# Routing four groups at a time, scaling x on ScalarE and VectorE, and copying x during the first stage

## The chip, the cores and the metric

One core of one Trainium2 chip runs the whole kernel. The metric is the device time of one execution in microseconds (us): the median of three runs. An engine's name is followed once by its short name in the profile: TensorE (PE; PEld is its weight load), VectorE (DVE), ScalarE (ACT), GpSimd (POOL), SyncE (SP, which here only issues DMAs).

## The reference

```python
# x [128, 64, 256], cond [128, 256], w [256, 256]; then T = 8192 tokens of D = 256, E = 8 experts, F = 1024
ys = y * (1 / sqrt(256))
d = rsqrt(einsum('bi,io->bo', ys * ys, w * w) + EPS)
hidden = einsum('bsi,io->bso', x * ys[:, None, :], w) * d[:, None, :]
logits = hidden @ wr.T                       # [T, 8]
vals, idx = top_k(logits, 2)                 # gating = softmax over the two
mask = (idx[:, :, None] == arange(E)).any(axis=1)
pos = cumsum(mask, axis=0) - 1               # place of a token in its expert's list
keep = mask & (pos < cap)                    # cap = 2560
dispatch[e, slot] = token                    # the list of each expert
h = gelu(xg @ w1[e] + b1[e]);  y = h @ w2[e] + b2[e]
out = x + segment_sum(y * g, dispatch)       # back to the tokens
```

Everything is float32. The order of the tokens matters: the cumulative count runs over all 8192 of them.

## The kernel before

There are two stages. The first makes `hidden` and the routing, for 16 groups of 512 tokens (`GROUPS`, four tiles of 128 each). The second runs the experts, in 46 blocks of 384 slots, each of 8 chunks of the inner dimension.

In the first stage each group passes through these steps.

- SP loads a group of x, transposed, into one of four buffers (`load_x`), and loads the next one into a buffer when `modulate` has read it.
- POOL multiplies it by `ys` in place, in two instructions (`scale_x`, L336), two groups ahead.
- PE multiplies by `w` (`modulate`, L464) into three banks.
- ACT scales the lower half by `d` (`scale_hidden`, L672, eight small instructions), DVE the upper half (L810).
- PE turns the group back to token rows and computes the logits at once (`turn_back`, L477 and L479); ACT copies the four tiles into `rows` (`copy_back`, L657).

The routing works on a set of two groups (`PAIR = 2`, so 8 tiles and 8 sets). DVE takes the two largest logits and their experts (`choose`, L820 to L834, a chain of small instructions, each of which waits for the one before). The difference goes to ACT for an exponential (`odds`, L662), and DVE makes the two gates (`set_gates`, L839 to L845) right behind `choose`. POOL writes the gates into `rows` (`weigh_gates`, L344 to L349), and SP stores the set to `hidden` in DRAM (`store_rows`). PE counts positions (`positions`, L489 to L500), DVE turns them into slot numbers (`find_slots`, L852 to L869), and for each group writes one-hot tiles (`list_group`, L876 and L890) that PE multiplies into the lists (`list_slots`, L511). VectorE's program is a loop over groups g: `scale_hidden(g)`; at even g `list_group(g-3)`, `choose` and `set_gates` of the set that ends with g-1; at odd g `find_slots` and `list_group(g-3)`; and for g from 3 to 10 one piece of the first expert's weights is split (`split_piece`, L779 on DVE, L648 on ACT). PE's is `modulate(g)`, at odd g `positions`, `turn_back(g-1)`, `list_slots(g-4)`.

At the end POOL works out what is added to the lists (`base_ids`, L371 to L380), DVE adds it (`ids`, shown as L790, a helper's line) and POOL gathers the rows of block 0 (`gather`, L391). SP loads the weights of expert 1 when the first expert's are split, and when all groups are listed it loads `b2` and issues 16 copies of x into the output (`copy_x`, L280), to which the second stage adds. PE transposes a gathered block (`transpose_block`, L537) and starts the products (L547 to L561). ACT applies gelu (L701), and in the first two blocks of an expert it also splits the next expert's weights, waiting for them before the first piece.

Of the kernel before, what the change touches and what calls it, by code (L numbers as in the profile page):

```python
# [30 lines left out]
PAIR = 2  # L31
SETS = GROUPS // PAIR
TS = PAIR * TILES
X_RING = 4
ROW_RING = 4
# [34 lines left out]
def build(nc, x, x_t, cond_t, w, wr_t, w1, b1_t, w2, b2, ident, tri, expert_low, slot_base, middle_ids, lanes,  # L70
# [9 lines left out]
    with ExitStack() as ctx:  # L80
# [36 lines left out]
        base_ids = sb("base_ids", [P, E, TILES_E])  # L117
# [15 lines left out]
        first = [sb(f"first{u}", RE) for u in range(2)]  # L133
        second = [sb(f"second{u}", RE) for u in range(2)]
# [9 lines left out]
        gate = [sb(f"gate{u}", [P, 2, TS]) for u in range(2)]  # L144
        picked = sb("picked", [P, 2, TS, E])
        weighed = sb("weighed", [P, 2, TS, E])
# [40 lines left out]
        set_act = sem("set_act")  # L187
        w_loaded = sem("w_loaded")

        x_loaded = [sem(f"x_loaded{i}") for i in range(X_RING)]  # L190
        xs_ready = sem("xs_ready")
# [11 lines left out]
        gates_ready = sem("gates_ready")  # L203
        gates_weighed = sem("gates_weighed")
# [3 lines left out]
        halves_known = sem("halves_known")  # L208
        half_saved = sem("half_saved")
        base_step = sem("base_step")  # L210
        base_ready = sem("base_ready")
# [63 lines left out]
        def _(sp):  # L275
# [14 lines left out]
            for g in range(1, X_RING):  # L290
                load_x(g)
            sp.wait_ge(set_dve, 1)
# [11 lines left out]
            for g in range(X_RING, GROUPS):  # L304
# [25 lines left out]
        def _(pool):  # L330
            def scale_x(g):

                pool.wait_ge(x_loaded[g % X_RING], 16 * (g // X_RING + 1))
                for k in range(KC):
                    cols = x_in[g % X_RING][:, k, :].rearrange("p (b s) -> p b s", s=S)
                    pool.tensor_tensor(cols, cols, ys_t[:, k, g * GB:(g + 1) * GB].unsqueeze(2).to_broadcast([P, GB, S]),  # L336
                                       ALU.mult).then_inc(xs_ready, 1)

            def weigh_gates(s):

                pool.wait_ge(gates_ready, s + 1)
                if s > 0:
                    pool.wait_ge(rows_ready, s)
# [11 lines left out]
            for g in range(GROUPS):  # L355
                if g + 2 < GROUPS:
                    scale_x(g + 2)
# [90 lines left out]
        def _(pe):  # L448
# [70 lines left out]
            for g in range(1, GROUPS):  # L519
# [6 lines left out]
                if g >= 4:  # L526
                    list_slots(g - 4)
# [539 lines left out]
```

## Time and profile before

| what | us |
|---|---|
| median of 3 runs | 1011.01 (1010.73 to 1012.35) |
| profiled execution, whole | 1011.03 |
| its span, first to last instruction | 1008.8 |
| PE busy | 935.2 (93%) |
| ACT busy | 511.7 (51%) |
| DVE busy | 489.3 (49%) |
| POOL busy | 439.5 (44%) |

The profile shows one execution. Times are from the span's start. The chain of work that ended last is followed back from the last instruction; 84% of it is PE. Busy time of PE says less than it seems, since matmuls are pipelined and their ends are modelled; the start of one to the start of the next is the measure that counts. The same holds for DVE and ACT: an instruction's duration includes a part that overlaps with the next.

### The profile page before, as it was taken

To read this page: it belongs to the slowest core of one execution; us is meant where nothing else is said; L and a number is where in the kernel's file an instruction comes from. 1 tells how busy PE (TensorE), PEld (TensorE's weight loads), DVE (VectorE), ACT (ScalarE), POOL (GpSimd) and SP (SyncE) were. 2 spreads that over 40 slices of the span, in tenths; PEclk is the share of its full clock that TensorE was granted. 3 is DMA by queue.
4 is the path that set the end of the run, shared out by engine and by line. 5 is a ranking of instruction groups with operands and counts; after the bars stand their busy time and mean duration, and the time that the engine had idled before them with its cause. 6 is when DMAs were issued, how large, how long until landed. Compare 5 with 4: busy or idle time off the path is not lost.

```text
span 1008.8 us, 19314 instructions
## 1 busy us (share of the span) xinstructions
PE 935.2 (93%) x6398; PEld 889.5 (88%) x6399; DVE 489.3 (49%) x1152; ACT 511.7 (51%) x1106; POOL 439.5 (44%) x480
## 2 busy tenths in 40 slices
PE   6887861999999999999999999999999999999994
PEld 3454540999999999999999999999999999999994
DVE  3678683453554346443544455345444544344441
ACT  3543330565565556555655556556455655545551
POOL 4142213253544545454454535445453544545433
PEclk9999985899999999999999999999999999999997
DMA  8434229552244323523252325323432232322322
GB/s 271 113 106 146 66 93 354 182 131 37 51 76 101 47 38 52 122 49 47 48 130 37 50 39 131 47 48 46 120 50 41 48 47 44 48 37 52 42 33 32
DMA packets 53466, 82.04 MB, mean 81 GB/s; under 512 B 6656, under 2 KB 42496, under 8 KB 53056
## 3 DMA queue, kind: packets, MB, share of 16 engines
q0 software_dynamic: 26496, 36.76, 23.3%
q1 hardware_dynamic: 25392, 44.42, 13.5%
q10 hardware_dynamic: 1552, 0.53, 0.2%
q8 instruction: 13, 0.21, 0.1%
q14 instruction: 13, 0.11, 0.0%
HBM read 54.16 MB, written 35.93 MB: 89 GB/s over the span
## 4 chain that ended last, share of the span: by engine, by line
PE 84%; DVE 9%; DMA 3%; issue 2%; POOL 1%; ACT 1%; SPq 0%; POOLq 0%; DVEq 0%
PE bank L559 13%; PE bank L560 13%; PE bank L561 13%; PE bank L548 13%; PE bank L547 13%; PE bank L549 13%; PE bank L537 3%; DMA sb_xg<-hidden,sb_gather_ids 2%; PE bank L464 1%; PE bank L477 1%; PE bank L479 1%; DVE sb_h_raw L890 1%; DVE sb_h_raw L876 1%; DVE sb_hid_t L810 1%; DVE sb_picked L860 1%
## 5 line engine op out<-in xcount | busy, mean ns | idle before, releaser
L969 DVE TENSOR_TENSOR sb_h_lo<-sb_h_raw,sb_h_hi 128x384 fp32r<-128x384 f32 x368 | 205.2, 558 | 321.5 <-ACT sb_h_hi L701 321.5
L701 ACT ACTIVATE sb_h_raw<-bank,sb_b_now 128x384 f32<-128x384 f32 x368 | 214.8, 584 | 282.2 <-PE bank L549 282.0
L559 PE MATMUL bank<-sb_w_hi,sb_h_hi 128*128 128x256 f32 x1104 | 315.1, 285 | 0.0
L560 PE MATMUL bank<-sb_w_lo,sb_h_hi 128*128 128x256 f32 x1104 | 311.6, 282 | 0.0
L561 PE MATMUL bank<-sb_w_hi,sb_h_lo 128*128 128x256 f32 x1104 | 310.1, 281 | 0.0
L404 POOL DMA_INDIRECT out_rows<-sb_y,sb_add_ids x138 | 222.8, 1614 | 67.8 <-POOL sb_add_ids L401 38.0
L547 PE MATMUL bank<-sb_xt_hi,sb_w_hi 128*128 128x384 f32 x736 | 250.0, 340 | 1.7 <-issue 1.7
L548 PE MATMUL bank<-sb_xt_lo,sb_w_hi 128*128 128x384 f32 x736 | 249.9, 340 | 0.0
L549 PE MATMUL bank<-sb_xt_hi,sb_w_lo 128*128 128x384 f32 x736 | 249.6, 339 | 0.0
L701 ACT ACTIVATE sb_h_hi<-bank,sb_b_now 128x384 fp32r<-128x384 f32 x368 | 212.3, 577 | 0.0
L561 PEld LDWEIGHTS bank<-sb_w_hi,sb_h_lo 128*128 128x128 f32 x1104 | 208.4, 189 | 0.0
L559 PEld LDWEIGHTS bank<-sb_w_hi,sb_h_hi 128*128 128x128 f32 x1104 | 208.0, 188 | 0.0
L560 PEld LDWEIGHTS bank<-sb_w_lo,sb_h_hi 128*128 128x128 f32 x1104 | 207.6, 188 | 0.0
L391 POOL DMA_INDIRECT sb_xg<-hidden,sb_gather_ids x138 | 136.8, 992 | 67.4 <-POOL sb_ids_ring L387 39.1
L547 PEld LDWEIGHTS bank<-sb_xt_hi,sb_w_hi 128*128 128x128 f32 x736 | 138.8, 189 | 2.1 <-issue 2.1
L548 PEld LDWEIGHTS bank<-sb_xt_lo,sb_w_hi 128*128 128x128 f32 x736 | 138.9, 189 | 0.0
L549 PEld LDWEIGHTS bank<-sb_xt_hi,sb_w_lo 128*128 128x128 f32 x736 | 138.9, 189 | 0.0
L386 POOL COPY sb_gather_ids<-sb_ids 128x3 int32 (+1 forms) x46 | 11.3, 247 | 265.6 <-DVE sb_gates L937 263.1
L690 ACT CAST sb_xt_hi<-bank 128x384 fp32r<-128x384 f32 x92 | 39.6, 483 | 111.3 <-PE bank L549 81.6
L928 DVE TENSOR_TENSOR sb_xt_lo<-bank,sb_xt_hi 128x384 fp32r<-128x384 f32 x92 | 47.1, 553 | 95.1 <-ACT sb_xt_hi L690 95.1
L994 DVE TENSOR_TENSOR sb_y<-bank,sb_b 128x256 f32<-128x256 f32 x138 | 50.1, 419 | 43.4 <-PE bank L561 43.4
L464 PE MATMUL bank<-sb_x,sb_w 128*128 128x512 f32 x128 | 63.8, 646 | 1.4 <-ACT sb_hid_t L672 1.4
(113 smaller groups left out, 622.0 us busy)
## 6 DMA issues: line engine op xcount, KB each, us to landing
sb_w_raw<-in_w SPq DMA_DIRECT2D x16, 1024.0 KB, 8.3
hidden<-sb_rows SPq DMA_DIRECT2D x8, 1056.0 KB, 6.3
sb_x<-in_x_t SPq DMA_DIRECT2D x16, 512.0 KB, 4.2
out_rows<-in_x SPq DMA_DIRECT2D x16, 512.0 KB, 14.1
sb_xg<-hidden,sb_gather_ids POOLq DMA_INDIRECT x138, 2.8
out_rows<-sb_y,sb_add_ids POOLq DMA_INDIRECT x138, 3.8
sb_b<-in_b SPq DMA_DIRECT2D x1, 1024.0 KB, 5.7
hidden<-sb_empty SPq DMA_DIRECT2D x3, 132.0 KB, 8.2
```

Of the source, the lines that this page charges most:

```text
L391: pool.indirect_dma_start(xg[:, s, :], None, hidden, bass.IndirectOffsetOnAxis(gather_ids[:, s:s + 1], axis=0),).then_inc(gathered, 16)
L404: pool.indirect_dma_start(out, bass.IndirectOffsetOnAxis(add_ids[:, s:s + 1], axis=0), y[s][:, :], None, compute_op=ALU.add,).then_inc(add ...
L464: mm = pe.matmul(m_bank[c % M_RING][:, :], w_sb[:, k, o * P:(o + 1) * P], x_in[g % X_RING][:, k, :], start=(k == 0), stop=(k == KC - 1))
L547: pe.matmul(h, w_hi[u][:, cols], xt_hi[:, rows], start=(k == 0), stop=False)
L548: pe.matmul(h, w_hi[u][:, cols], xt_lo[:, rows], start=False, stop=False)
L549: mm = pe.matmul(h, w_lo[u][:, cols], xt_hi[:, rows], start=False, stop=(k == KC - 1))
L559: pe.matmul(y, hi, w_hi[u][:, cols], start=(f == 0), stop=False)
L560: pe.matmul(y, hi, w_lo[u][:, cols], start=False, stop=False)
L561: mm = pe.matmul(y, lo, w_hi[u][:, cols], start=False, stop=(f == FC - 1))
L701: ins = act.activation(h, h_bank[f % H_BANKS][:, 0:SLOTS], ACT.Gelu_apprx_tanh, bias=b1_now[u][:, f:f + 1])
L969: dve.tensor_tensor(h_lo[f % RING][:, :], h_raw[f % RING], h_hi[f % RING][:, :].bitcast(F32), ALU.subtract).then_inc(h_ready, 1)
L994: dve.tensor_tensor(y[s][:, :], y_bank[s][:, 0:D], b2_sb[:, bass.ds(e * D, D)], ALU.add).then_inc(y_read, 1)
```

## The change

`JOINED = 4` takes the place of `PAIR = 2`: four groups, 16 tiles, are one set, and there are four sets. The instructions of `choose`, `set_gates`, `find_slots` and `positions` are issued half as often on twice the width; `rows` has two buffers of twice the size. `set_gates` stands a group after `choose`, behind `find_slots`, and DVE also writes the gates to `rows`. The scaling of x leaves POOL: ACT does the lower half in eight small instructions, DVE the upper half in one. DVE also does POOL's work on the list base, after its last group, and `b2` is waited for later. SP issues one copy of x behind each load of x; the load of `b2` and of expert 1's weights now stands behind the first transposes of the second stage (`t_done`). The table of the square root is loaded ahead of its use.

```diff
-PAIR = 2
-SETS = GROUPS // PAIR
+JOINED = 4
+SETS = GROUPS // JOINED
-ROW_RING = 4
+ROW_RING = 2
@@ sync
+            sp.wait_ge(zeros, 1)
...
-                if g % 2 == 0 and g >= 8:
-                    store_rows((g - 8) // 2)
-            for s in range(GROUPS // 2 - 4, SETS):
-                store_rows(s)
+                copy_x(g - X_RING)
+                if g % JOINED == 2 and g >= 2 * JOINED:
+                    store_rows(g // JOINED - 2)
+            store_rows(SETS - 2)
+            for g in range(GROUPS - X_RING, GROUPS):
+                copy_x(g)
+            store_rows(SETS - 1)
+            sp.wait_ge(t_done, 1)
+            sp.dma_start(b2_sb[:, :], b2.rearrange("e d -> (e d)").partition_broadcast(P)).then_inc(b2_in, 16)
             sp.wait_ge(w_lo_done, PIECES)
             load_weights(1)
-            sp.wait_ge(listed, GROUPS)
-            sp.dma_start(b2_sb[:, :], b2.rearrange("e d -> (e d)").partition_broadcast(P)).then_inc(b2_in, 16)
-            for g in range(GROUPS):
-                copy_x(g)
@@ gpsimd: scale_x, weigh_gates and the work on base_ids go
@@ tensor
-                pe.wait_ge(xs_ready, KC * (g + 1))
+                pe.wait_ge(xs_lower, g + 1)
+                pe.wait_ge(xs_upper, g + 1)
...
-                if g >= 3 and g % 2 == 1:
-                    positions((g - 3) // 2)
+                if g % JOINED == 1 and g > JOINED:
+                    positions(g // JOINED - 1)
                 turn_back(g - 1)
-                if g >= 4:
-                    list_slots(g - 4)
+                if g % JOINED == 3 and g > JOINED:
+                    list_slots(g - 7)
+                    list_slots(g - 6)
+                if g % JOINED == 0 and g > JOINED:
+                    list_slots(g - 6)
+                    list_slots(g - 5)
             turn_back(GROUPS - 1)
-            list_slots(GROUPS - 4)
+            list_slots(GROUPS - 6)
+            list_slots(GROUPS - 5)
             positions(SETS - 1)
-            for g in range(GROUPS - 3, GROUPS):
+            for g in range(GROUPS - JOINED, GROUPS):
                 list_slots(g)
@@ scalar
+            def scale_x(g):
+
+                act.wait_ge(x_loaded[g % X_RING], 16 * (g // X_RING + 1))
+                for i in range(GB):
+                    cols = x_in[g % X_RING][:, 0, i * S:(i + 1) * S]
+                    b = g * GB + i
+                    ins = act.mul(cols, cols, ys_t[:, 0, b:b + 1])
+                ins.then_inc(xs_lower, 1)
...
             for g in range(GROUPS):
+                if g + 2 < GROUPS:
+                    scale_x(g + 2)
                 if g + 1 < GROUPS:
                     scale_hidden(g + 1)
+                if g % JOINED == 0 and g > 0:
+                    odds(g // JOINED - 1)
                 copy_back(g)
-                if g % 2 == 0 and g >= 2:
-                    odds(g // 2 - 1)
@@ vector
+            def scale_x(g):
+
+                dve.wait_ge(x_loaded[g % X_RING], 16 * (g // X_RING + 1))
+                cols = x_in[g % X_RING][:, 1, :].rearrange("p (b s) -> p b s", s=S)
+                dve.tensor_tensor(cols, cols, by_batch(ys_t, 1, g), ALU.mult).then_inc(xs_upper, 1)
...
             for g in range(GROUPS):
                 scale_hidden(g)
-                if g == GROUPS // 2 + 4:
-                    dve.wait_ge(listed, GROUPS // 2)
-                    dve.tensor_copy(lower_list[:, :], list_half[0]).then_inc(half_saved, 1)
-                if g % 2 == 0:
-                    if g >= 4:
-                        list_group(g - 3)
-                    if g >= 2:
-                        choose(g // 2 - 1)
-                        counts = set_gates(g // 2 - 1)
-                elif g >= 3:
-                    find_slots((g - 3) // 2, counts)
-                    list_group(g - 3)
+                if g + 2 < GROUPS:
+                    scale_x(g + 2)
                 if 3 <= g < 3 + PIECES:
                     split_piece(0, g - 3, g - 2)
+                if g == GROUPS // 2 + 5:
+                    save_half()
+                if g % JOINED == 0 and g > 0:
+                    choose(g // JOINED - 1)
+                if g % JOINED == 1 and g > JOINED:
+                    find_slots(g // JOINED - 1)
+                    set_gates(g // JOINED - 1)
+                if g % JOINED == 2 and g > JOINED:
+                    list_group(g - 6)
+                    list_group(g - 5)
+                if g % JOINED == 3 and g > JOINED:
+                    list_group(g - 5)
+                    list_group(g - 4)
             choose(SETS - 1)
             set_gates(SETS - 1)
-            list_group(GROUPS - 3)
-            find_slots(SETS - 1, None)
+            find_slots(SETS - 1)
+            for g in range(GROUPS - JOINED, GROUPS):
+                list_group(g)
```

## Rows read from the trace of the kernel before

**Rows 1.** Busy time by stretch: each engine's us (instructions), granted clock, DMA share, GB/s.

```profile
60.39:78.13 17.74, 14.51 (x73) 9.22 (x73) 14.20 (x38) 7.65 (x27) 5.29 (x7) 0.92 0.40 119
...
160.00:190.00 30.00, 12.32 (x66) 11.95 (x67) 6.74 (x17) 8.04 (x17) 6.32 (x8) 0.62 1.00 342
```

**Rows 2.** Timeline of DVE over one set: start, duration, instruction [idle before].

```profile
61.59 0.68 DVE L876 TENSOR_TENSOR sb_h_raw<-sb_lanes,sb_lane_of 128x1024 f16<-128x1024 f16 x1
...
63.56 0.22 DVE L820 TENSOR_REDUCE sb_top<-sb_rows 128x8 f32<-128x64 f32 x1
...
66.38 0.22 DVE L834 TENSOR_TENSOR sb_mask<-sb_first,sb_second 128x64 bf16<-128x64 f32 x1
69.57 0.17 DVE L839 TENSOR_SCALAR sb_gate<-sb_ratio 128x8 f32<-128x8 f32 x1 [2.96 <-ACT sb_ratio L662]
...
70.74 0.68 DVE L810 TENSOR_TENSOR sb_hid_t<-bank,sb_d_t 128x512 f32<-128x512 f32 x1
71.34 0.22 DVE L852 TENSOR_SCALAR sb_over<-bank 128x64 f32<-128x64 f32 x1
...
76.15 0.69 DVE L876 TENSOR_TENSOR sb_h_raw<-sb_lanes,sb_lane_of 128x1024 f16<-128x1024 f16 x1
```

**Rows 3.** Timeline of POOL over the same set.

```profile
71.58 4.08 POOL L336 TENSOR_TENSOR sb_x<-sb_x,sb_ys_t 128x512 f32<-128x512 f32 x4
```

**Rows 4.** Timeline of DVE where POOL no longer scales x.

```profile
139.88 0.21 DVE L852 TENSOR_SCALAR sb_over<-bank 128x64 f32<-128x64 f32 x1
...
141.92 0.69 DVE L876 TENSOR_TENSOR sb_h_raw<-sb_lanes,sb_lane_of 128x1024 f16<-128x1024 f16 x1
```

**Rows 5.** Timeline of PE in the same set as Rows 2.

```profile
66.66 0.20 PE L495 MATMUL bank<-sb_mask,sb_tri 128*128 128x64 bf16 x1 [0.48 <-DVE sb_mask L834]
...
66.91 0.47 PE L477 MATMUL bank<-sb_back,sb_hid_t 128*128 128x136 f32 x2
...
68.85 1.38 PE L511 MATMUL bank<-sb_b,sb_h_raw 128*128 128x168 f16 x8
70.05 3.61 PE L464 MATMUL bank<-sb_x,sb_w 128*128 128x512 f32 x8
73.50 0.40 PE L477 MATMUL bank<-sb_back,sb_hid_t 128*128 128x136 f32 x2
```

**Rows 6.** Timeline of ACT in the same set.

```profile
72.04 1.75 ACT L672 ACTIVATE sb_hid_t<-bank,sb_d_t 128x64 f32<-128x64 f32 x8 [2.00 <-PE bank L464]
74.16 1.77 ACT L657 COPY sb_rows<-bank 128x264 f32<-128x264 f32 x4 [0.37 <-PE bank L479]
```

**Rows 7.** Timeline of DVE at the start.

```profile
6.33 1.34 DVE L759 TENSOR_TENSOR sb_wsq<-sb_w 128x512 f32<-128x512 f32 x1
...
15.39 0.42 DVE L771 TENSOR_TENSOR sb_d_t<-sb_tmp_t,sb_root_t 128x256 f32<-128x256 f32 x1
```

**Rows 8.** Timeline of PE: the last matmuls of the last `turn_back`.

```profile
141.76 0.40 PE L479 MATMUL bank<-sb_back,sb_hid_t 128*128 128x136 f32 x2
```

**Rows 9.** Timeline of DVE: the list is complete.

```profile
158.96 0.33 DVE L790 TENSOR_TENSOR sb_ids<-bank,sb_base_ids 128x168 int32<-128x168 f32 x1 [1.58 <-PE bank L511]
```

**Rows 10.** Timeline of SP's queue: the issue of the 16 copies of x.

```profile
159.24 10.59 SPq L280 DMA_DIRECT2D out_rows<-in_x x16
```

**Rows 11.** The chain that ended last: block 0's gather from its last issue, and its transposes.

```profile
163.38 12.52 DMA sb_xg<-hidden,sb_gather_ids
175.94 1.55 PE bank L537 x6
```

**Rows 12.** The page's DMA issues: count, KB each, median us from issue to landing.

```profile
hidden<-sb_rows SPq DMA_DIRECT2D x8, 1056.0 KB, 6.3
...
sb_xg<-hidden,sb_gather_ids POOLq DMA_INDIRECT x138, 2.8
```

**Rows 13.** Timeline of ACT in block 0: its first piece of expert 1's weights.

```profile
185.24 0.62 ACT L648 CAST sb_w_hi<-sb_w_raw 128x512 fp32r<-128x512 f32 x1
```

**Rows 14.** Timeline of PE in block 0: the product of chunk 6 starts.

```profile
190.47 0.34 PE L547 MATMUL bank<-sb_xt_hi,sb_w_hi 128*128 128x384 f32 x1
```

More of the change, by code:

```diff
@@ L132, in build @@
         hit = sb("hit", RE)
-        first = [sb(f"first{u}", RE) for u in range(2)]
-        second = [sb(f"second{u}", RE) for u in range(2)]
+        chosen = sb("chosen", [P, 2, TS, E])
+        first, second = chosen[:, 0, :, :], chosen[:, 1, :, :]
         mask = sb("mask", RE, BF16)
@@ L143, in build @@
         ratio = sb("ratio", [P, TS])
-        gate = [sb(f"gate{u}", [P, 2, TS]) for u in range(2)]
+        gate = sb("gate", [P, 2, TS])
         picked = sb("picked", [P, 2, TS, E])
-        weighed = sb("weighed", [P, 2, TS, E])
         slot_of = sb("slot_of", [P, 2, TS])
@@ L330, in _ @@
         def _(pool):
[L331 to L343, printed above, removed]
-                pool.tensor_tensor(weighed[:, 0, :, :], first[s % 2][:, :, :],
-                                   gate[s % 2][:, 0, :].unsqueeze(2).to_broadcast(RE), ALU.mult)
-                pool.tensor_tensor(weighed[:, 1, :, :], second[s % 2][:, :, :],
-                                   gate[s % 2][:, 1, :].unsqueeze(2).to_broadcast(RE), ALU.mult).then_inc(gates_weighed, 1)
-                pool.wait_ge(gates_weighed, s + 1)
-                pool.tensor_tensor(rows[s % ROW_RING][:, :, GATE_AT:GATE_AT + E], weighed[:, 0, :, :],
-                                   weighed[:, 1, :, :], ALU.add).then_inc(rows_ready, 1)
@@ L640, in _ @@
             act.dma_start(lane_sb[:, :, :], lanes.rearrange("p (n j) -> p n j", j=TILES)).then_inc(const_in, 16)
+            act.wait_ge(zeros, 1)
+            act.activation(warm_sb[:, :], empty_sb[:, 0:1], ACT.Sqrt)
+            def scale_x(g):
[5 more added lines that the diff above has]
+                ins.then_inc(xs_lower, 1)
+            act.wait_ge(set_dve, 2)
+            scale_x(0)
+            scale_x(1)
             act.wait_ge(set_dve, 5)
@@ L823, in choose @@
                 after(mark(dve.tensor_reduce(low[:, 0, :], hit[:, :, :], AX_X, ALU.min)))
-                after(mark(dve.tensor_tensor(first[s % 2][:, :, :], low3, over_e(low[:, 0, :]), ALU.is_equal)))
-                after(mark(dve.scalar_tensor_tensor(rest[:, :, :], first[s % 2][:, :, :], -BIG, logits,
+                after(mark(dve.tensor_tensor(first, low3, over_e(low[:, 0, :]), ALU.is_equal)))
+                after(mark(dve.scalar_tensor_tensor(rest[:, :, :], first, -BIG, logits,
                                                     ALU.mult, ALU.add)))
@@ L990, in one_block @@
                     split_chunk(b + 1, 0)
+                if isinstance(b, int) and b == 0:
+                    dve.wait_ge(b2_in, 16)
                 for s in range(SUBS):
```

114 lines of the change are left out of this document (50 added, 64 removed).

## The prediction

> **What bounds the kernel now.** I read the busy time by stretch first. From 200 us on PE never idles and the change touches nothing there, so the question is how early the second stage starts. In the first stage [rows 1], over one set of two groups (17.74 us), DVE is busy 14.20, PE's records 14.51 at a granted clock of 0.92, ACT 7.65. That settles nothing, so I followed DVE's timeline through the set [rows 2], from start to start: `list_group` 1.97 (61.59 to 63.56), `choose` 3.04 (63.56 to 66.60), idle 2.96 for ACT's exponential, `find_slots` 4.81 (71.34 to 76.15), `scale_hidden` 0.60. With the second list, the second hidden, two weight pieces (0.60 each) and gates (0.57) that is 17.7: DVE's own order fills the period, 8.87 us a group. Two parts are not work. The 2.96 us is a wait: ACT's exponential stands behind `copy_back`, that behind PE's `turn_back`, that behind `positions`, which waits for the mask (0.48) [rows 5]. And `find_slots` takes 4.81 beside POOL's four scalings of x [rows 3], but 2.04 where POOL has none [rows 4]: 2.77 us.
>
> PE's own work [rows 5]: `modulate` 3.45 (70.05 to 73.50), `turn_back` 1.94 at most (66.91 to 68.85; 1.85 by its steps of 0.23), `list_slots` 1.20 (68.85 to 70.05), `positions` 0.25 a set of two. So 6.6 us a group: DVE costs 2.2 us a group over PE.
>
> The end of the stage: the last `turn_back` ends at 142.0 [rows 8] (141.76 plus its second half), the list is complete at 159.3 [rows 9], and then block 0's gather takes 12.52 us from its last issue [rows 11], while all 16 copies of x go out from 159.24 [rows 10] and the DMA engines are full, 342 GB/s [rows 1]. The same gather lands in 2.8 us as a rule [rows 12]. PE stands still for all of it.
>
> **DVE after the change.** A small instruction of `choose` steps by 0.25 us; 64 more elements at DVE's pace, read off the 0.60 us step of a 512-element one and the 0.25 step of a 64-element one (448 elements, 0.35 to 0.45 us), are 0.06. Per set of four groups: `choose` 3.04 + 12 x 0.06 = 3.8; `find_slots` 2.04 + about 0.8 = 2.8 (two 64-wide products become one of 256); gates with the two instructions that were POOL's 1.45; four lists 7.9; four `scale_hidden` 2.4; four halves of `scale_x` at the same width 2.4; weight pieces 2.4. Sum 23.2, and 20.8 once the pieces are done: 5.8 and 5.2 us a group. The exponential has a whole group of time, so the 2.96 goes; POOL is silent, so the 2.77 goes.
>
> **PE sets the pace then.** Per four groups: 4 x (3.45 + 1.85 + 1.20) = 26.0, and `positions` for 16 tiles. That is 1216 columns in place of 352 (sum of its matmul widths) against 0.25 us: 0.6 to 0.9, I take 0.6. So 26.6 us per set of four, 6.65 a group, uneven: 5.3, 5.9, 7.7, 7.7, since lists come at g mod 4 = 3 and 0. Does anything miss its turn? The mask of a set: its last rows are copied 5.9 us into iteration 4k, `choose` ends at 9.8, and `positions` is asked at 7.7 + 3.45 = 11.1: 1.3 us spare, but for the first set, with no lists yet, 1.0 late. Lists are made by 23.3 and asked at 24.2.
>
> **ACT.** Hidden 8 x 0.20 = 1.62 (the 1.75 of [rows 6] less the tail), `copy_back` 1.66, and the new `scale_x`. No row shows a 64-wide scaling out of SBUF. Bounds: as out of PSUM, 1.62, or without any overlap at 0.33 each, 2.66. I take 1.62, the same form on the same engine. Then 4.9 a group, 5.4 with a weight piece: under 6.65, but even with PE's 5.3 in groups that have no lists.
>
> **The start.** `wsq` takes 1.34 beside POOL [rows 7], and 0.68 is what a product of that width takes alone [rows 2]; two of the 256-wide steps on the way to `d` are slowed likewise. Against that ACT must scale groups 0 to 2 itself before hidden. I take `d` 2.4 us earlier than 15.8, and after ACT's added 1.7 us `modulate(2)` at 19.5 instead of 21.3.
>
> **The first stage summed.** `modulate(2)` at 19.5. Groups 2 to 6 at 5.4 to 5.6 (ACT and PE even), with the first `positions` 0.6 and its late mask 1.0: `modulate(7)` at 48.3. Then 7.7, 7.7, 5.9, 5.4, 7.7, 7.7, 5.9, 5.4: `modulate(15)` at 101.7, its iteration's end 109.4, last `turn_back` 111.3. Before, 142.0. Saved 30.7.
>
> **The tail** grows. From the end of that `turn_back`: copy 0.7, `choose` 3.8, gates 1.5, `find_slots` 3.0 with its wait for `positions`, four lists 7.9 where two stood, PE's last list 1.4, the `ids` 0.5: 18.8. DVE's five steps for the base fit beside the last list. Before it was 159.3 - 142.0 = 17.3. Net 29.2: the list is complete at 130.1.
>
> **The gather.** The rows of the last set must be stored first. That store is 2.1 MB, issued at about 117.3; the 1056 KB one lands in 6.3 [rows 12], and another 1.1 MB at 342 GB/s or at half of that adds 3.2 to 6.3, so it lands between 126.8 and 130. The first gather is issued at 131.4: hidden by 1.4 to 4.6 us. With the copies gone, the gather lands in 2.8 instead of 12.5: 9.7 saved. Landing of block 0's rows: 175.9 - 29.2 - 9.7 = 137.0.
>
> The Trainium skill, "DMA: Bandwidth & Descriptors", § Queues, rings and completion order, says that a DMA's semaphore increment lands only after every earlier write of that DMA engine, across its queues. By it the 12.5 us is the wait behind copies that were issued before the gather, and [rows 10, 11] fit; it would also put the gather behind the store of the last set, should that be late.
>
> **A new wait in block 0.** SP now issues `b2` (1 MB) and expert 1's weights (2 MB) behind the first transposes, which end 1.6 us after the landing [rows 11]. With block 1's rows 3.55 MB go out; at 342 GB/s 10.4 us, and up to 2.8 more for completion: they are there 12.5 to 15.3 us after the landing. ACT wants them 9.3 after it (185.24) [rows 13], so it stalls 3 to 6 us. PE wants the gelu behind that piece at 14.6 (190.47) [rows 14], and ACT needs 0.5 + 1.1 us from the weights to it: late by 0 to 2.3. I take 1.4; later pieces are not late. The `b2` wait of DVE is later still and costs nothing.
>
> **Sum.** 1008.8 - 29.2 - 9.7 + 1.4 = 971.3 of span. Around the span the profiled execution has 2.2 us (1011.03), and it stands at the median (1011.01): 973.5, I say 974.
>
> **Rivals.**
> 1. *ScalarE becomes the bound.* For it: only 0.1 to 0.5 us spare in groups without lists. If a scaling out of SBUF costs up to 0.33 us, ACT takes 6.4 with a weight piece and 5.9 without. Groups 2 to 6 then cost 4 to 5 us more, and each later short pair 0.5 to 1 us: 6 in all, 980; the full bound gives 984. Against: ACT has 1 to 2 us spare in each pair of 7.7.
>    The Trainium skill, "VectorE: DVE Perf Modes", § The TRN2 errata, gives ScalarE 224 fixed cycles from SBUF and 172 from PSUM; as an estimate from that page, 43 ns on each of 128 instructions, 5.5 us of ACT, would by this rival's reckoning make it some 976 to 977. No row here can show it.
> 2. *The gather was not held by the copies* but by its own first use or by the last store, which is now twice as large: the 9.7 us stays. 974 + 9.7 = 984. The change would not do that half of what it says. Against: [rows 1, 10].
> 3. *Transfers bound the first stage.* One queue now carries load, copy and store: 0.52 + 0.52 + 0.54 MB = 1.6 MB a group. At 342 GB/s that is 4.7 us, under 6.65. But a store of 1056 KB in 6.3 us is no more than 170 GB/s, completion included [rows 12]. Stores alone at that rate and the rest at 342 make 6.3 us: still under. Should it be at 220 GB/s throughout, 7.3 us a group: 8 us more, 982 to 990.
> 4. *Slower than before.* The same mechanism further on: every x load stands behind a copy and a store, and all traffic runs at the store's 170 GB/s. From 1.6 MB / 9.3 us, that is under 172 GB/s, the first stage eats the whole 37 us; at 160 GB/s it is 10 us a group, 1021. Against: 342 GB/s with 16 copies in flight [rows 1].
> 5. *Better than I count:* DVE and ACT start earlier and no weights stall: 963 to 968.
>
> **How the numbers follow.** Forecast (966 to 979) 0.60; ScalarE bound (979 to 984) 0.14; gather unchanged (984) 0.07; transfers (982 to 990, a tail above) 0.10; slower 0.02; better 0.07. A measurement of this kernel tells about 0.2% (2 us) from no change. The range 966 to 986 leaves out the better case, the slower one and most of the tail, 0.15 or so. Faster 0.97, same 0.01, slower 0.02.
>
> **What would show it.** PE's waits in the first stage all but gone, clock near 1.00, `modulate` to `modulate` at 5.3, 5.9, 7.7, 7.7; `modulate(15)` near 102; DVE waiting for PE; the list complete near 130; the gather landing in about 3 us; ACT waiting 3 to 6 us for weights in block 0. Wrong if: ACT has no idle time in groups 2 to 8 (rival 1); DVE or ACT waits for loads of x (3, 4); the last issue of the first gather to its landing stays near 12 (2); or the set's mask, not PE, releases `positions` in each set.

## The result, and the profile after

The changed kernel takes 976.02 us, the median of four executions (974.30 to 976.37), against 1011.27 for the kernel before on the same chip. The ratio is 0.9647, with a 95% interval of 0.9630 to 0.9663: 35 us faster. The profiled execution took 976.05, its span is 974.2 (before: 1008.8). The forecast of 974 was 2 us low, and the range held the result.

Where the 34.6 us of span come from: the list is complete at 134.7 instead of 159.3 (24.6 us), and block 0's rows land 6.8 us after that, where they took 16.6 before (9.8). From the landing to the end both kernels take the same, 832.7 and 832.9.

First the view by stretch of the kernel after, which answers [rows 1]. Its columns: stretch, length, then busy us (instructions) of PE, PEld, DVE, ACT and POOL, granted clock of TensorE as a share of 2.4 GHz, DMA share, GB/s.

```profile
42.70:47.09 4.39, 4.19 (x33) 4.19 (x34) 1.34 (x3) 1.84 (x5) 0.00 (x0) 0.61 0.55 212
47.09:114.50 67.41, 67.41 (x358) 44.74 (x357) 56.07 (x131) 51.73 (x201) 0.00 (x0) 1.00 0.61 206
```

From 47.09 to 114.50, ten iterations, PE is never idle and its clock is granted in full: 6.74 us a group, where it was 8.87. DVE is busy 83% and ACT 77% of it, so both still have room. The first row is the one stretch in the middle of the stage where this fails; it comes back below.

The timeline of PE of the kernel after, one set of four groups, `modulate` (L411) from start to start, and the set's first count of positions (L442), which answer [rows 5]. Columns: start, duration, instruction, tiles, [idle before].

```profile
60.56 3.61 PE L411 MATMUL bank<-sb_x,sb_w 128*128 128x512 f32 x8
...
68.30 3.62 PE L411 MATMUL bank<-sb_x,sb_w 128*128 128x512 f32 x8
...
71.75 0.22 PE L442 MATMUL bank<-sb_mask,sb_tri 128*128 128x128 bf16 x1
...
74.27 3.17 PE L411 MATMUL bank<-sb_x,sb_w 128*128 128x512 f32 x7
```

The steps are 7.74 and 5.97 (the last line is short because its view ends there), and `positions` waits for nothing, since DVE has written the mask 0.3 us before it is asked (71.17 and 0.29 long, next fence). The timeline of DVE of the kernel after over `choose` of the same set, against [rows 2]:

```profile
67.61 0.28 DVE L797 TENSOR_REDUCE sb_top<-sb_rows 128x16 f32<-128x128 f32 x1
...
71.17 0.29 DVE L811 TENSOR_TENSOR sb_mask<-sb_chosen 128x128 bf16<-128x128 f32 x1
72.02 0.69 DVE L789 TENSOR_TENSOR sb_hid_t<-bank,sb_d_t 128x512 f32<-128x512 f32 x1 [0.56 <-PE bank L411]
```

`choose` for 16 tiles takes 3.8 us (67.61 to 71.38), as forecast, and behind it DVE waits for PE: the roles have changed. No wait for the exponential is left.

The chain that ended last of the kernel after, in order of time, from the first gather to the first transposes, against [rows 11]:

```profile
136.02 1.17 POOL sb_xg L337
...
138.77 2.72 DMA sb_xg<-hidden,sb_gather_ids
141.50 0.04 issue
141.54 1.54 PE bank L489 x6
```

The gather lands 2.72 us after its last issue, where it took 12.52.

### The profile page after: what moved, and what is told of

It is laid out like the page before. It is cut to its first block, busy times and chain, and to the rows that moved or that the text cites. A ratio compares the mean times of both kernels' runs of the same rounds, so it can differ in the third digit from the quotient of the medians.

```text
span 974.2 us, 19276 instructions
## 1 busy us (share of the span) xinstructions
PE 932.7 (96%) x6402; PEld 891.0 (91%) x6403; DVE 470.1 (48%) x1068; ACT 539.6 (55%) x1231; POOL 390.7 (40%) x419
## 4 chain that ended last, share of the span: by engine, by line
PE 84%; issue 14%; POOL 1%; DMA 0%; DVE 0%; POOLq 0%; DVEq 0%
PE bank L511 14%; PE bank L512 14%; PE bank L513 13%; PE bank L499 13%; PE bank L500 13%; PE bank L501 13%; PE bank L489 3%; POOL out_rows L350 0%; DMA sb_xg<-hidden,sb_gather_ids 0%; POOL sb_xg L337 0%; DVE sb_y L997 0%; DVE sb_y L1003 0%; POOL sb_add_ids L347 0%; POOL sb_gather_ids L332 0%; POOL sb_ids_ring L333 0%
## 5 line engine op out<-in xcount | busy, mean ns | idle before, releaser
L511 PE MATMUL bank<-sb_w_hi,sb_h_hi 128*128 128x256 f32 x1104 | 314.8, 285 | 0.0
L511 PEld LDWEIGHTS bank<-sb_w_hi,sb_h_hi 128*128 128x128 f32 x1104 | 207.8, 188 | 0.0
L411 PE MATMUL bank<-sb_x,sb_w 128*128 128x512 f32 x128 | 59.5, 608 | 0.5 <-ACT sb_hid_t L639 0.4
```

The source lines that it names most:

```text
L411: mm = pe.matmul(m_bank[c % M_RING][:, :], w_sb[:, k, o * P:(o + 1) * P], x_in[g % X_RING][:, k, :], start=(k == 0), stop=(k == KC - 1))
L511: pe.matmul(y, hi, w_hi[u][:, cols], start=(f == 0), stop=False)
```

## The experiments

Each time below is a median with the range of its runs, beside the kernel before on the same chip (1011.8 to 1012.4 in the four sessions). Comparisons across sessions go by the ratios.

### The copies of x alone, added to the kernel before

```diff
+                copy_x(g - X_RING)
                 if g % 2 == 0 and g >= 8:
                     store_rows((g - 8) // 2)
+            for g in range(GROUPS - X_RING, GROUPS):
+                copy_x(g)
             for s in range(GROUPS // 2 - 4, SETS):
                 store_rows(s)
...
-            for g in range(GROUPS):
-                copy_x(g)
```

> The kernel before with one part of the change: the copies of x go out one behind each load of x in the first stage; everything else stays, so b2 and expert 1's weights are issued where they were. Theory (the copies alone held the first gather, and the first stage has room for their traffic): the gather lands in about 3 us from its last issue instead of 12.52, the list is complete at 159 us as before, and the kernel is 9 to 10 us faster, ratio 0.990. Rival (the gather is held by its own first use or by the store and weight transfers ahead of it): it still takes 8 us or more and the kernel gains under 4 us. Rival (the copies cost the first stage what they give to the gather): the list is complete several us later.

Measured: 1002.2 us (1001.47 to 1004.41) against 1012.26, ratio 0.9909 (0.9892 to 0.9926). The chain that ended last of this kernel:

```profile
164.08 2.83 DMA sb_xg<-hidden,sb_gather_ids
166.90 0.04 issue
166.95 1.54 PE bank L538 x6
```

The list comes at about the same time (160.0 against 159.3), and the gather lands 2.83 us after its last issue. So the 12.52 us came from the copies, and neither from the gather's first use nor from the last store; the copies' new place is worth 9.2 us (by the ratio) to 10.1 us (by the medians) by itself.

### The reverse: the changed kernel with its transfers ordered as before

```diff
-                copy_x(g - X_RING)
...
-            for g in range(GROUPS - X_RING, GROUPS):
-                copy_x(g)
             store_rows(SETS - 1)
-            sp.wait_ge(t_done, 1)
-            sp.dma_start(b2_sb[:, :], ...)
             sp.wait_ge(w_lo_done, PIECES)
             load_weights(1)
+            sp.wait_ge(listed, GROUPS)
+            sp.dma_start(b2_sb[:, :], ...)
+            for g in range(GROUPS):
+                copy_x(g)
```

> The kernel after, with the order of the transfers as before the change: expert 1's weights right behind the last store of rows, then b2 and all 16 copies once the lists are complete. Theory (the copies' part of the change is worth the 9.8 us by which the gather lands sooner, and the first stage does not feel them): the list is complete at 134 to 135 us as with them, the gather takes about 12 us from its last issue, and the kernel is 9 to 10 us slower than the one after: 985 to 986. Rival (the copies delay the first stage's loads or stores by some us): the list comes earlier and the difference is under 7 us.

Measured: 984.24 us (984.06 to 986.62), ratio 0.9733 (0.9716 to 0.9749), against 0.9647 with the copies spread. The chain that ended last of this kernel:

```profile
136.96 11.06 DMA sb_xg<-hidden,sb_gather_ids
148.02 0.04 issue
148.06 1.55 PE bank L488 x6
```

The gather is back at 11.06 us. The first stage of this kernel is not faster for having no copies in it: PE starts each `modulate` within 0.2 us of the kernel with them up to the first `positions`, and after it is 1.8 us ahead, 1.7 of it for another reason (the clock, below). So the 8 MB of copies cost the first stage 0.2 us at most, and rival 3, transfers as its bound, falls. The two experiments agree: by the ratios the copies' early place is worth 9.2 us in the kernel before and 8.7 here (0.0086), or up to 10.4 with the 1.7 that the clock takes in one profiled execution and not in the other.

The Trainium skill, "DMA: Bandwidth & Descriptors", § Queues, rings and completion order, has a DMA's semaphore increment wait for all earlier writes of that DMA engine, in whatever queue. Four gathers agree: 12.52 and 11.06 us with the copies issued ahead, 2.83 and 2.72 without. The runs don't tell this rule from a gather that merely shares the DMA engines with the copies; both would end with the copies moved.

### The gates a group later, in the kernel before

```diff
                         choose(g // 2 - 1)
-                        counts = set_gates(g // 2 - 1)
                 elif g >= 3:
+                    counts = set_gates((g - 3) // 2)
                     find_slots((g - 3) // 2, counts)
```

> The kernel before with only this: VectorE makes the gates of a set in the odd group, ahead of find_slots, instead of right behind choose. Theory (VectorE's own order sets the period of the first stage, and its wait for ScalarE's exponential is a whole part of it): the 2.96 us wait goes in 7 sets, about 20 us, less what PE then asks: 1011 - 15 to 20 = 991 to 996. Rival (the wait only moves, because another engine is as late: the rows that POOL weighs and x that POOL scales behind it now come later): under 8 us, and a new wait of the same length stands in VectorE's or PE's timeline.

Measured: 1007.62 us (1006.74 to 1009.25), ratio 0.9953 (0.9936 to 0.9970): 4.6 us, and the theory fell. The timeline of DVE of this kernel, gates and `find_slots`:

```profile
68.40 0.17 DVE L839 TENSOR_SCALAR sb_gate<-sb_ratio 128x8 f32<-128x8 f32 x1 [1.89 <-ACT sb_ratio L662]
...
70.33 0.85 DVE L865 TENSOR_SCALAR sb_near<-sb_slot_of 128x16 f32<-128x16 f32 x1
71.22 0.96 DVE L866 TENSOR_SCALAR sb_col_of<-sb_near 128x16 f16<-128x16 f32 x1
72.22 0.97 DVE L869 SCALAR_TENSOR_TENSOR sb_lane_of<-sb_col_of,sb_slot_of 128x16 f16<-128x16 f16 x1
73.22 1.48 DVE L876 TENSOR_TENSOR sb_h_raw<-sb_lanes,sb_lane_of 128x1024 f16<-128x1024 f16 x1
```

Of the 2.96 us of wait 1.89 is left: moving the reader does little while ACT's exponential still stands behind `copy_back`. The next rows show how POOL slows DVE. Its four scalings run from 70.12 for 4.04 us (1.01 each, timeline of POOL), and four DVE instructions step by 0.89, 1.00, 1.00 and 1.41, though three of them have only 16 elements a partition (0.21 without POOL). Each of these four loses 0.7 to 0.8 us, whatever its width. Not every instruction does: in the kernel before, a reduction from 128 to 16 elements beside the same scalings takes 0.29 us (L861 at 74.78), as it does without them.

```profile
70.12 4.04 POOL L336 TENSOR_TENSOR sb_x<-sb_x,sb_ys_t 128x512 f32<-128x512 f32 x4
```

The Trainium skill, "SBUF — State Buffer", § Who interferes with whom, describes this as an exclusive lock on the port pair that DVE shares with GpSimd, not as shared bandwidth. The steps agree with it.

### The gates later, and the exponential ahead of the copies

```diff
-                copy_back(g)
                 if g % 2 == 0 and g >= 2:
                     odds(g // 2 - 1)
+                copy_back(g)
...
                 if s < SETS - 1:
+                    dve.wait_ge(mask_ready, s + 1)
```

This is on top of the edit before. The added wait belongs to it: the count in `set_gates` reads the mask, and once the exponential no longer stands behind `copy_back`, nothing else orders that read behind the write.

> The kernel before with the gates made in the odd group and ScalarE's exponential ahead of its copy_back. The run with the gates alone gained 4.6 us and left 1.89 us of wait for the exponential in each set. Theory (the exponential still stood behind copy_back, that behind PE's turn_back; only both moves take the wait away): VectorE's wait is gone, the period of a set falls from 16.9 to about 15.0 us, 11 to 13 us below the run with the gates alone, so about 995. Rival (POOL's scaling falls on other instructions and takes it back, or PE or ScalarE is late instead): the period stays above 16.3 us and the kernel above 1003.

Measured: 992.46 us (991.49 to 993.57) against 1012.24, ratio 0.9807 (0.9792 to 0.9822). The timeline of PE of this kernel at two successive counts of positions:

```profile
60.57 0.20 PE L495 MATMUL bank<-sb_mask,sb_tri 128*128 128x64 bf16 x1 [1.25 <-DVE sb_mask L834]
...
75.50 0.20 PE L495 MATMUL bank<-sb_mask,sb_tri 128*128 128x64 bf16 x1 [1.31 <-DVE sb_mask L834]
```

A set of two now takes 14.93 us instead of 17.74, and from the second set on DVE doesn't wait for the exponential (in the first it waits 0.89). Two lines in another order are worth 20 us, with POOL still scaling x: the largest part of the whole gain.

### POOL's scaling of x left out

```diff
-                for k in range(KC):
-                    cols = x_in[g % X_RING][:, k, :]...
-                    pool.tensor_tensor(cols, cols, ..., ALU.mult).then_inc(xs_ready, 1)
+                pool.sem_inc(xs_ready, KC)
```

> The kernel before without the scaling of x by ys (that part of the computation is left out; POOL only passes the group on). Theory (POOL's scaling doubles the time of VectorE's two-input instructions beside it, 2.77 us in each find_slots): find_slots takes 2.0 to 2.3 us in every set instead of 4.8, the first stage is 6 x 2.8 = 17 us shorter, and at the start wsq takes 0.69 instead of 1.34 us; in all 15 to 20 us faster, 991 to 996. Rival (find_slots is slow for a reason of its own, such as reading PSUM while PE writes): it stays over 4 us and the kernel gains under 4 us.

Measured: 974.35 us (974.20 to 974.79), ratio 0.9629, but this total says little. With x unscaled the tokens are routed otherwise, and the second stage has 45 blocks instead of 46 (135 gathers instead of 138), 17.5 us by the stretch from landing to end (815.4 against 832.9). What can be compared is the first stage. There a set takes 14.91 us instead of 17.74, the 2.8 that the prediction read off `find_slots`, whose part up to `list_group` now takes 1.98 us (63.81 to 65.79). The timeline of DVE of this kernel:

```profile
62.04 0.17 DVE L836 TENSOR_SCALAR sb_gate<-sb_ratio 128x8 f32<-128x8 f32 x1 [2.96 <-ACT sb_ratio L659]
...
63.81 0.21 DVE L849 TENSOR_SCALAR sb_over<-bank 128x64 f32<-128x64 f32 x1
...
65.37 0.17 DVE L863 TENSOR_SCALAR sb_col_of<-sb_near 128x16 f16<-128x16 f32 x1
65.58 0.18 DVE L866 SCALAR_TENSOR_TENSOR sb_lane_of<-sb_col_of,sb_slot_of 128x16 f16<-128x16 f16 x1
65.79 0.69 DVE L873 TENSOR_TENSOR sb_h_raw<-sb_lanes,sb_lane_of 128x1024 f16<-128x1024 f16 x1
```

The wait for the exponential stays at 2.96: it and the contention are two separate costs, as the prediction had it.

### The scaling of x moved to ScalarE and VectorE, in the kernel before

```diff
+            def scale_x(g):     # ACT: lower half, eight act.mul; DVE: upper half, one tensor_tensor
...
             for g in range(GROUPS):
+                if g + 2 < GROUPS:
+                    scale_x(g + 2)
```

> The kernel before with one part of the change: ScalarE scales the lower half of x, VectorE the upper half, POOL none; sets of two groups, gates and copies as before. Theory (a set's find_slots loses the 2.77 us that POOL costs it, and VectorE pays 2 x 0.60 for its halves): the period of a set falls from 17.7 to 16.2 us, six to seven sets, the start is the same within 1 us: 9 to 11 us faster, 1001 to 1003. Rival (ScalarE's added 1.9 us a group delay its copy_back and with it the exponential that VectorE waits for): that wait grows past 2.96 us and the gain is under 5 us.

Measured: 1006.48 us (1004.62 to 1008.41), ratio 0.9937 (0.9918 to 0.9956): 6 us, less than expected. The timelines of ACT and DVE of this kernel, the first copy of one set and the gates of that set and of the next:

```profile
67.24 0.38 ACT L658 COPY sb_rows<-bank 128x264 f32<-128x264 f32 x1 [3.29 <-PE bank L468]
...
70.30 0.17 DVE L851 TENSOR_SCALAR sb_gate<-sb_ratio 128x8 f32<-128x8 f32 x1 [4.63 <-ACT sb_ratio L663]
...
86.57 0.17 DVE L851 TENSOR_SCALAR sb_gate<-sb_ratio 128x8 f32<-128x8 f32 x1 [2.96 <-ACT sb_ratio L663]
```

DVE is rid of the contention, 2.8 us a set, and pays 1.2 for its halves of x. Where TensorE's clock stays full, its wait for the exponential is still 2.96 and a set takes 16.27 us (masks at 49.18 and 65.45, and again at 83.39 and 99.66), as the theory had it; the rival's longer wait doesn't come. What took part of the gain back is the clock. PE now pauses 1.91 us for the mask, and behind two of those pauses its clock fell to half (last section): then the four copies step by 0.90, the wait is 4.63 and 4.62, and the set takes 17.94 us (65.45 to 83.39) or 17.56. That is some 3 us in all, and the start is 2.2 us later as well; with both, the 6 us would be 11, the upper end of what was expected.

### All of it with sets of two

The four edits above put together in the kernel before, so with the scaling, the copies, the exponential and the gates all moved:

```diff
 PAIR = 2
...
+                if g + 2 < GROUPS:
+                    scale_x(g + 2)
...
+                copy_x(g - X_RING)
...
-                copy_back(g)
                 if g % 2 == 0 and g >= 2:
                     odds(g // 2 - 1)
+                copy_back(g)
...
+                    counts = set_gates((g - 3) // 2)
                     find_slots((g - 3) // 2, counts)
```

POOL still writes the gates into the rows and makes the list base.

> The kernel before with all parts of the change but the sets of four (and the small ones that hang on them): x scaled by ScalarE and VectorE, gates in the odd group, the exponential ahead of copy_back, copies of x spread over the first stage; sets stay at two groups, POOL still writes the gates and the list base. What it tells: what the sets of four are worth. VectorE's sum for two groups is then 3.95 + 3 x 1.2 + 3.04 + 0.57 + 2.04 = 13.2 us with weight pieces and 12.0 without; PE's is 2 x 6.5 + 0.25 = 13.2. Theory (PE sets the pace either way, and the wide instructions only give VectorE room): the period is 13.3 to 14 us a set of two, against 26.9 a set of four in the kernel after, and the tail is 1 us shorter: 975 to 980, within 4 us of the kernel after. Rival (with both engines even every wait for the mask is PE's, and the clock falls behind it): period 14.9 or more, 985 to 990.

Measured: 975.63 us (975.05 to 977.47) against 1012.40, ratio 0.9638 (0.9620 to 0.9657), the same as the changed kernel's 0.9647 (0.9630 to 0.9663). The busy time by stretch of this kernel:

```profile
60.00:110.00 50.00, 49.90 (x276) 33.48 (x275) 45.25 (x142) 40.18 (x151) 3.78 (x12) 1.00 0.75 243
```

And its timeline of PE at two successive counts of positions, neither of which waits:

```profile
59.18 0.20 PE L485 MATMUL bank<-sb_mask,sb_tri 128*128 128x64 bf16 x1
...
72.58 0.20 PE L485 MATMUL bank<-sb_mask,sb_tri 128*128 128x64 bf16 x1
```

DVE is busier than with sets of four (45.25 of 50 us against 41.20 in the same stretch), as twice the number of small instructions should make it. It doesn't matter, since PE is busy 49.90 of 50: 13.40 us a set of two, 6.70 a group. Sets of four buy nothing that can be measured once the rest is in. Nor do they with their first set's late mask out of the way, which sets of two don't have: that kernel's ratio is 0.9621 (below), 1.7 us better than this one's, with intervals that overlap.

### More work for ScalarE in the changed kernel

```diff
+                for i in range(4):
+                    ins = act.mul(spare_sb[:, i * S:(i + 1) * S], ys_t[:, 0, 0:S], ys_t[:, 0, i:i + 1])
```

Four unused scalings of 64 elements a group, 1.0 us.

> The kernel after with four more scalings of 64 elements on ScalarE in each group, ahead of scale_hidden (their results are not used). They cost it 4 x 0.24 = 1.0 us a group. Theory (PE sets the pace; ScalarE is even with it in the groups that have no lists, and has 1.4 to 2 us spare where lists stand): groups 2 to 6, 9, 10, 13 and 14 pay up to 1.0 each, those with lists nothing: 7 to 10 us slower, 983 to 986. Rival (ScalarE is not near the bound anywhere): under 3 us slower. Rival (ScalarE is the bound in every group): 14 to 16 us slower, 990 to 992.

Measured: 983.7 us (983.3 to 984.54), ratio 0.9719 (0.9704 to 0.9734), some 7.3 us over the changed kernel. The timeline of PE of this kernel:

```profile
22.93 3.60 PE L413 MATMUL bank<-sb_x,sb_w 128*128 128x512 f32 x8
28.87 3.60 PE L413 MATMUL bank<-sb_x,sb_w 128*128 128x512 f32 x8
...
49.43 3.60 PE L413 MATMUL bank<-sb_x,sb_w 128*128 128x512 f32 x8
55.88 3.60 PE L413 MATMUL bank<-sb_x,sb_w 128*128 128x512 f32 x8
...
61.77 0.50 PE L426 MATMUL bank<-sb_back,sb_hid_t 128*128 128x136 f32 x2 [0.90 <-ACT sb_rows L626]
...
64.77 3.61 PE L413 MATMUL bank<-sb_x,sb_w 128*128 128x512 f32 x8
```

Groups without lists pay: 5.94 instead of 5.28, and 6.45 instead of 5.52 with a weight piece. Of the two groups with lists in a set only the second stays (7.75 for 7.74). The first pays 0.94 (55.88 to 64.77, 8.89 for 7.95): its `turn_back` waits for ACT's copy of the short group before, so the short group's lateness reaches into it. The theory had both paying nothing. ACT is even with PE in the short groups, as the prediction had it, and one group behind them; rival 1 is true there.

### Three orders mended in the changed kernel, one by one and together

The count behind `turn_back`, so that the first set's late mask stops nothing:

```diff
+                turn_back(g - 1)
                 if g % JOINED == 1 and g > JOINED:
                     positions(g // JOINED - 1)
-                turn_back(g - 1)
```

> The kernel after, with PE's positions behind turn_back instead of ahead of it, in the groups where it stands. In the trace of the kernel after PE waits 2.06 us for the first set's mask and its clock then falls to 0.60 for 4.3 us. Theory (that stall and the clock that falls behind it are the 3 us by which the first stage missed the forecast): both go, the first four groups' set costs PE nothing, and the kernel is 2 us (where the clock had not fallen) to 4 us faster than the one after: 972 to 974. Rival (VectorE, which reads the positions 1.9 us later, is late with its lists): a wait of PE for the lists comes instead, and the time is the same within 1 us.

Measured: 973.97 us (973.74 to 974.24), ratio 0.9621 (0.9608 to 0.9634). `modulate(6)` starts at 44.92 instead of 47.09, and the clock is granted in full around it. The stall doesn't go, though. The timeline of PE of this kernel:

```profile
43.74 0.50 PE L424 MATMUL bank<-sb_back,sb_hid_t 128*128 128x136 f32 x2 [1.50 <-ACT sb_rows L624]
```

PE now waits 1.50 us in `turn_back` for ACT's copy of the group before. A kernel with the old order and a full clock (expert 1's weights early, below) starts `modulate(6)` at 45.45, so 0.5 of the 2.2 us is the order and the rest the clock.

ACT's square root ahead of its scaling of group 1:

```diff
             scale_x(0)
-            scale_x(1)
             act.wait_ge(set_dve, 5)
             act.activation(root_t[:, :], var_t[:, :], ACT.Sqrt).then_inc(set_act, 1)
+            scale_x(1)
```

> The kernel after, with ScalarE's root ahead of its scaling of group 1 (8 instructions, 1.9 us). Theory (the scaling in front of the root is why d comes 1.4 us later than forecast): d comes 1.4 us earlier; but ScalarE then scales group 1 while VectorE works on d, so that product waits for it, and group 2 starts about 1.4 us earlier: 974.6. Rival (PE or ScalarE sets the start, not d): under 0.5 us.

Measured: 974.56 us (973.25 to 975.02), ratio 0.9625 (0.9612 to 0.9638). The timeline of DVE, the reciprocal that waits for the root, in the changed kernel and then in this one:

```profile
11.50 1.75 DVE L742 RECIPROCAL sb_root_t<-sb_root_t 128x256 f32<-128x256 f32 x1 [1.78 <-ACT sb_root_t L609]
```

```profile
10.18 1.75 DVE L742 RECIPROCAL sb_root_t<-sb_root_t 128x256 f32<-128x256 f32 x1 [0.48 <-ACT sb_root_t L608]
```

The wait is 1.3 us shorter, and `modulate(2)` starts 1.3 us earlier (19.83 instead of 21.16).

Expert 1's weights ahead of the last store:

```diff
+            sp.wait_ge(w_lo_done, PIECES)
+            load_weights(1)
             store_rows(SETS - 1)
             sp.wait_ge(t_done, 1)
             sp.dma_start(b2_sb[:, :], ...)
-            sp.wait_ge(w_lo_done, PIECES)
-            load_weights(1)
```

> The kernel after, with the load of expert 1's weights ahead of the last store of rows instead of behind the first transposes. Theory (the 3.35 us that ScalarE waits for weights in block 0 are covered by PE's queue of opened products, since PE asked for the gelu only at the moment when it was done): ScalarE's wait goes, and the time stays within 0.7 us of the kernel after. Rival (the wait costs what I forecast): 1.4 us faster. Rival (2 MB ahead of or beside the last store delay it past the first gather): slower by 2 to 6 us.

Measured: 974.38 us (973.91 to 976.19), ratio 0.9630 (0.9616 to 0.9643). ACT no longer waits for weights, and from landing to end it is 832.0 us against 832.7. That is 0.7 at most, and nothing that the totals can tell. Of it 0.5 is already there when PE starts the first product with gelu's output (L511, 9.13 us after the landing against 9.60), before any of the awaited weights is used.

None of the three intervals is clear of the changed kernel's. The last kernel has all three edits:

> The kernel after with the three small moves together: positions behind turn_back, the root ahead of the scaling of group 1, expert 1's weights ahead of the last store. Each alone ran at 974.0 to 974.6. In their traces the positions' move takes 2.5 us at the list's end and keeps the clock from falling (some executions of the kernel after lose 1.8 us there), the root's move takes 1.4, the weights' 0.7. Theory (they are independent): 974.3 (the kernel after without the fall of the clock) - 0.4 - 1.4 - 0.7 = 971.8. Rival (they share one slack): 973 to 974.

Measured: 972.64 us (972.03 to 973.36) against 1012.24, ratio 0.9609 (0.9596 to 0.9622). This interval lies below that of the changed kernel: some 3.8 us by the ratios, and the fastest version that was run.

## Why the prediction held, point by point

**What bounded the kernel.** Right, and shown. The wait for the exponential and POOL's contention together set the 17.74 us of a set: undoing both (with x scaled by ACT and DVE) takes it to 13.40, and undoing one to 14.9, by either way. That the two don't add is also plain: after either of them DVE needs under 7.5 us a group, and the other has only 0.8 us a group to win before PE sets the pace.

**PE sets the pace.** Forecast 26.6 us a set of four, measured 27.19 and 26.97 (52.61, 79.80 and 106.77 for `modulate` 7, 11 and 15). Each step came out within 0.1 to 0.2 of what was said, 7.74 for a group with lists, 5.97 with `positions`, 5.53 and 5.29 without either, and 7.95 for the first group with lists of a set, whose `turn_back` takes 2.09 instead of 1.86, all of it at the fourth tile. The term was 0.4 to 0.6 too small.

**The start** is the term that was mis-sized most: `d` at 14.96 where 13.4 was forecast, `modulate(2)` at 21.16 for 19.5. Two steps failed. I took 2.4 us of gain out of POOL's silence, and it is 2.0: with POOL's scaling left out `d` is there at 13.78 instead of 15.81. And I said nothing of the square root's place: ACT scaled group 1 first, and DVE waited 1.78 us. The experiment gets 1.3 of it back. The reciprocal takes 1.75 us beside POOL and without it; only the products had been slowed.

**The first set.** Its late mask was forecast at 1.0 us and is 2.06. DVE's weight piece stands ahead of `choose` and waits for ACT's half of it. What no step had was what follows. The timeline of PE of the changed kernel, and then that of the changed kernel with the copies late:

```profile
42.90 0.23 PE L442 MATMUL bank<-sb_mask,sb_tri 128*128 128x128 bf16 x1 [2.06 <-DVE sb_mask L811]
...
44.09 0.66 PE L426 MATMUL bank<-sb_back,sb_hid_t 128*128 128x136 f32 x2
44.55 0.66 PE L424 MATMUL bank<-sb_back,sb_hid_t 128*128 128x136 f32 x2
```

```profile
42.73 0.23 PE L441 MATMUL bank<-sb_mask,sb_tri 128*128 128x128 bf16 x1 [2.05 <-DVE sb_mask L810]
...
43.65 0.40 PE L425 MATMUL bank<-sb_back,sb_hid_t 128*128 128x136 f32 x2
43.88 0.39 PE L423 MATMUL bank<-sb_back,sb_hid_t 128*128 128x136 f32 x2
```

After a pause of 2.06 us a pair of matmuls steps by 0.46 in the one execution, and after 2.05 by 0.23 in the other: the granted clock of that stretch is 0.61 there, 1.00 here. `turn_back` takes 3.6 us instead of 1.85, a loss of 1.7. Of the five profiled executions of kernels that have this pause the clock fell in one. Together the start, the mask, the clock and the steps make `modulate(15)` 5.1 us late (106.77 for 101.7).

**The tail** was forecast at 18.8 us from the last `turn_back` to the list and took 18.3 (116.36 to 134.7), so it gave 0.5 of the 5.1 back. The saving up to the list is 24.6 us and not 29.2: the one large error of the sum.

**The gather** was right: 2.72 us for 2.8. The last store was issued at 122.29 and takes 9.2 us to land by the page's median, about 131.5, ahead of the first gather at 136.02.

**The wait in block 0** was right in size and wrong in price. The timeline of ACT of the changed kernel, against [rows 13]:

```profile
154.66 0.62 ACT L615 CAST sb_w_hi<-sb_w_raw 128x512 fp32r<-128x512 f32 x1 [3.35 <-DMA sb_w_raw<-in_w]
```

It waits 3.35 us (forecast 3 to 6), but the product of chunk 6 starts at 156.42, 14.93 us after the landing against 14.57 before [rows 11, 14], and PE waits for nothing on the way. The 0.36 is not the weights' either: it is there in full at PE's first product with gelu's output (L511, and L559 before), 9.60 us after the landing against 9.24, because the first products ran at half clock for longer (granted 0.50 from 144.7 to 149.3; before, from 179.2 to 182.8). The step that failed is the price: I had charged 1.4 for a wait that cost PE nothing.

**The sum.** Forecast 29.2 + 9.7 - 1.4 = 37.5 of span; measured 24.6 + 9.8 + 0.2 = 34.6. The errors are small beside the 37 us, and most of them lie at the start and in the first set, where nothing has reached its steady order; the tail, block 0 and the gather gave 2.2 of the 5.1 back. That they did is luck, and so is part of the closeness of 974.

**The rivals.** ScalarE is even with PE in the groups without lists, and its lateness there reaches the first group with lists. Its scaling out of SBUF steps by 0.24 us (2.02 for eight), between the bounds 0.20 and 0.33. The Trainium skill, "VectorE: DVE Perf Modes", § The TRN2 errata, gives ScalarE 224 fixed cycles from SBUF and 172 from PSUM, as an estimate from that page 43 ns. The traces agree: 2.02 against 1.75 us for eight, 34 ns each, and steps of 0.24 against 0.20. The gather held by something else, transfers as the bound, and their slower end on the other side of zero are excluded by the first two experiments.

**Attribution.** Measured as pairs, the copies are worth 9 to 10 us; the order of gates and exponential 20 by itself; moving x 6 by itself, and in the last step, from 992.46 with the copies' 9 to 10 taken off to 975.63, 7 to 8; sets of four nothing that these runs can tell.

## What to carry to other kernels

When one engine waits in each round for another, look at what stands ahead of the awaited instruction in the other's queue, and move that instruction, not only its reader: here one such line was worth more than widening every instruction of the chain. Before batching to save instructions, ask which engine sets the pace afterwards; once that was PE, halving DVE's small work bought nothing here. Bulk copies that nobody waits for belong where the queues have room: here the gather that was issued behind them landed after 12.52 us instead of 2.8.

## What the runs showed of the hardware that was not expected

- After a pause of about 2 us TensorE's clock fell to half in some executions and not in others, with the same instructions around it: 2.06 us in the changed kernel (granted 0.61), but 2.04 or 2.05 with the copies late, the root first, the weights early or more work for ScalarE (1.00 in each). In one execution of the kernel with x moved there are four pauses of 1.91 or 1.92 us: the full clock follows the first and the third, half the clock the second and the fourth. The second and the third (view by stretch of that kernel):

```profile
65.77:69.58 3.81, 3.81 (x26) 3.80 (x26) 0.00 (x0) 1.14 (x3) 0.00 (x0) 0.55 0.29 108
83.71:85.85 2.14, 2.14 (x26) 2.14 (x26) 0.00 (x0) 1.02 (x3) 0.00 (x0) 1.00 0.49 189
```

  The same 26 matmuls take 3.81 and 2.14 us. It may also spread the times: the changed kernel's runs lie 2.1 us apart, those of the two kernels that pause only 1.50 us there 0.5 and 1.3. That the clock is the reason is not shown.
- Three DVE instructions of 16 elements a partition cost 0.9 to 1.0 us each beside POOL's scalings, against 0.21 alone, and one of 1024 elements 1.41 against 0.60: 0.7 to 0.8 us on each, whatever its width. A reduction beside them cost nothing extra (0.29).
- A reciprocal of 128x256 float32 takes 1.75 us on DVE, a product of that size 0.42.
- The load of the exponential's table took 1.28 us (41.90, timeline of ACT of the changed kernel), just before the first set's gates, and cost nothing there.
